# A two-layer language-model tower: quantised feed-forward and recurrence rebuilt as three streaming blocks, weights rounded beside the attention, expert mixture in quarters

## What is computed

```python
x = emb[inp]                        # token attention, then a second "spin" attention
# quantised feed-forward
scale = sigmoid(clip_x) * max(abs(x)) / 127         # one number for the whole tensor
xq = clip(round(x / scale), -128, 127) * scale
gate, up = xq @ q(w_gate).T, xq @ q(w_up).T         # q(): a scale for each row of w
h  = silu(gate) * up                                # 704 wide, then quantised like x
y  = h_q @ q(w_down).T
# recurrence with a mixture of 8 experts
x = inputs * rsqrt(mean(inputs * inputs) + 1e-6) * norm_weight
probs = softmax(mean(x, axis=1) @ router_w.T + router_b)   # one row for each sequence
W_hg, W_out = einsum(probs, w_hg), einsum(probs, w_out)
hidden, gate = split(x @ W_hg.T)                    # then the scan over 1024 steps
h_t = (1 - sigmoid(gate_t)) * h_{t-1} + sigmoid(gate_t) * g(hidden_t)
out = h @ W_out.T + inputs
# then 6 layers of local attention (16 heads, window 64) and a gated feed-forward
```

## Time and profile before

| | us |
|---|---|
| median of 3 runs (lowest, highest) | 4348.81 (4348.57, 4349.60) |
| the profiled execution, its own time | 4352.46 |
| its span in the profile | 4350.7 |
| second attention's last context | 1048.99 |
| scale of x known | 1121.02 |
| scale of h known | 1171.29 |
| shares of the experts known | 1262.67 |
| X for the local layers ready | 1367.27 |
| local layers' first matmul | 1375.30 |

### The profile page before, as it was taken

The page is one execution under the profiler, slowest core; times in us unless marked ns, Lnnn a source line. Parts: engine busy times, 40 slices in busy tenths (PEclk is TensorE's granted clock), DMA queues, the critical chain, the costliest instruction groups (busy, mean ns, idle before and its releaser), DMA issues. The chain is left out here.

```text
span 4350.7 us, 98162 instructions
## 1 busy us (share of the span) xinstructions
PE 4037.7 (93%) x33170; PEld 2814.9 (65%) x33172; DVE 3164.0 (73%) x5506; ACT 2640.2 (61%) x7021; POOL 1908.4 (44%) x1269
## 2 busy tenths in 40 slices
PE   6999979997426999999999999999999999999997
PEld 3666546664113677777777777777777777777776
DVE  4888448885865777777777777777777777777774
ACT  2677536774302666666666666666666666666664
POOL 1000000000002666666656666665666666566662
PEclk8999989999668999999999999999999999999999
DMA  6111141221022100111002100111002100111001
GB/s 154 40 44 44 23 114 44 55 55 32 0 69 96 23 20 19 50 45 27 20 19 61 39 20 21 49 45 27 20 19 60 40 19 21 49 47 25 20 19 49
DMA packets 102633, 178.80 MB, mean 41 GB/s; under 512 B 26756, under 2 KB 61472, under 8 KB 101792
## 3 DMA queue, kind: packets, MB, share of 16 engines
q1 hardware_dynamic: 101408, 170.87, 14.7%
q0 software_dynamic: 768, 2.10, 0.3%
HBM read 96.10 MB, written 23.07 MB: 27 GB/s over the span
## 5 line engine op out<-in xcount | busy, mean ns | idle before, releaser
L1855 POOL TENSOR_TENSOR swp<-raw,table 128x512 f32<-128x512 f32 x384 | 480.8, 1274 | 638.9 <-DVE ss L2266 638.8
L1017 DVE TENSOR_REDUCE maxima<-PS 128x1 f32<-128x512 f32 x1024 | 632.2, 680 | 123.8 <-PE PS L851 123.3
L1938 PE MATMUL PS<-wqk,xT 128*128 128x512 f32 x1536 | 687.7, 601 | 5.6 <-DMA wqk<-in_L_ffn_Wqkv 4.4
L1885 POOL TENSOR_TENSOR probs<-probs,prob_recip 128x512 f32<-128x512 f32 x384 | 476.4, 1260 | 430.4 <-DVE prob_recip L2324 430.4
L981 ACT ACTIVATE probs<-PS 128x512 f32<-128x512 f32 x1024 | 520.0, 603 | 155.2 <-PE PS L865 154.7
L2195 ACT ACTIVATE probs<-probs,neg 128x128 f32<-128x128 f32 x1536 | 595.9, 389 | 27.2 <-DVE neg L2318 25.7
L1865 POOL TENSOR_TENSOR rinv<-ssm,power 128x32 f32<-128x32 f32 x96 | 526.8, 5488 | 0.0
L1938 PEld LDWEIGHTS PS<-wqk,xT 128*128 128x128 f32 x1536 | 284.0, 190 | 336.8 <-issue 254.1
L2041 PE MATMUL PS<-xnT,w 128*128 128x128 f32 x3840 | 477.3, 276 | 0.4 <-DVE hidden L2384 0.4
L851 PE MATMUL PS<-k_stack,q_stack 112*128 112x512 f32 (+1 forms) x1024 | 430.8, 442 | 35.0 <-PEq L384 18.5
L2266 DVE TENSOR_REDUCE ss<-swp 128x16 f32<-128x1024 f32 x192 | 232.9, 1213 | 304.8 <-ACT swp L2146 304.8
(11 more groups left out here) (255 smaller groups left out, 8029.7 us busy)
## 6 DMA issues: line engine op xcount, KB each, us to landing
V_window<-V SPq DMA_DIRECT2D x180, 256.0 KB, 2.8
wqk<-in_L_ffn_Wqkv SPq DMA_DIRECT2D x12, 1024.0 KB
w<-in_L_ffn_W SPq DMA_DIRECT2D x18, 640.0 KB, 4.4
q_stack<-spin_qk SPq DMA_DIRECT2D x128, 80.0 KB
k_stack<-spin_qk SPq DMA_DIRECT2D x128, 80.0 KB
q_stack<-tok_qk SPq DMA_DIRECT2D x128, 64.0 KB
k_stack<-tok_qk SPq DMA_DIRECT2D x128, 64.0 KB
wv<-in_L_ffn_Wqkv SPq DMA_DIRECT2D x6, 1024.0 KB, 5.0
```

The source lines that it names most:

```text
L1017: dve.tensor_reduce(maxima[:, k // 2, k % 2:k % 2 + 1], SM(r, k), AX.X, ALU.max).then_inc(sm_maxed, 1)
L1855: pool.tensor_tensor(swp[:, w, :, a:a + LD // 2], raw[:, w, :, b:b + LD // 2], table[:, j % 2, 2 + w, a:a + LD // 2].rearrange("p (o d) -> ...
L1885: pool.tensor_tensor(view, view, psr[:, 4 * q:4 * q + 4].rearrange("p (h o) -> p h o", o=1) .to_broadcast([P, 4, P]), ALU.mult).then_inc(p ...
L1938: mm = pe.matmul(wide(kind, half, j), xT[:, k, at:at + P], rhs, start=(k == 0), stop=(k == DC - 1))
```

## The change

The chain of blocks between the second attention and the local layers becomes three blocks. `join_outputs` does the output projection, the layer norm, the peak and the turning of the weights; `feed_forward` does the quantised feed-forward, the layer norm, the second norm and the router; the new `recurrence` mixes, scans, projects, normalises and spills. In each, pairs of tiles or chunks pass from engine to engine.

- Weights: `QuantisedWeights` keeps 3072 + 1408 columns of weights; `beside` hooks in `attend` load them (SP, step 5), add the output bias to H (POOL, step 5), take the exponential of the clips (ACT, step 33) and round them (DVE, `round`, ahead of step 34). The last subtraction goes to ACT in `join_outputs`.
- Quantising h: ACT scales it and adds the rounding constant (1536 columns for a pair of tiles), DVE clips (L1536), ACT takes the constant off.
- POOL adds the down projection to H, computes both standard deviations from the moments (six small operations for each pair), and joins H and X.
- The router's weights are turned on the host, its logits come from PE; norm_weight goes into the experts' shares.
- Mixture: `w_hg` is mixed a quarter at a time by DVE (`mix(n)` for unit n: 2 + 14 operations of 2x128 columns), `w_out` by ACT (products) and POOL (14 sums of 128x512). The first unit's matmuls wait for its quarter only.
- All eight experts' weights are loaded at the start of `feed_forward`.
- One of the five cleanups goes; the one after the first attention moves to behind the second attention's projections.

```diff
+        with nc.cleanup_on_exit():
+            with ExitStack() as weights:
+                m = QuantisedWeights(c, weights, shared)
+                attend(c, V, qs, ks, second, spin_loaded, context, HD + 4, {
+                    "pool": {0: lambda pool: m.clear(c, pool), RING - 1: lambda pool: m.add_bias(c, pool, w["next"]["bo"])},
+                    "sp": {RING - 1: lambda sp: m.load(c, sp)},
+                    "act": {ITERS + 1: lambda act: m.exponent(c, act)},
+                    "dve": {ITERS + 2: lambda dve: m.round(c, dve)}})
+                join_outputs(c, context, w["next"]["wo"], m)
...
     def over_heads(eng, step, last, others):
...
+            if t in others:
+                others[t](eng)
...
+def join_outputs(c, context, wo, m):
...
+            @block.vector
+            def _(dve):
...
+                for ch in range(CHUNKS):
+                    add_output(2 * ch)
+                    add_output(2 * ch + 1)
+                    count(ch)
+                    if ch:
+                        norm(ch - 1)
+                norm(CHUNKS - 1)
...
+def feed_forward(c, m, x):
...
+            @block.gpsimd
+            def _(pool):
+                pool.memset(hT[64:P, IC - 1, :], 0.0).then_inc(cleared, 1)
...
+                def add_output(g):
+                    pool.wait_ge(out_scaled, g + 1)
+                    at = slice(PAIR * g, PAIR * g + PAIR)
+                    pool.tensor_tensor(c.H[:, at, :], c.H[:, at, :], scaled_out[:, g % 2, :, :], ALU.add).then_inc(ffn_added, 1)
...
+                def join(g):
+                    at = slice(PAIR * g, PAIR * g + PAIR)
+                    pool.wait_ge(normed, PAIR * g + PAIR)
+                    pool.tensor_tensor(c.H[:, at, :], c.H[:, at, :], c.X[:, at, :], ALU.add).then_inc(h_joined, 1)
+
+                for g in range(PAIRS + 1):
+                    if g < PAIRS:
+                        add_output(g)
+                        deviations(g)
+                    if g:
+                        join(g - 1)
...
+                for g in range(PAIRS + 2):
+                    if g + 1 < PAIRS:
+                        to_integers(g + 1)
+                    if g < PAIRS:
+                        round_h(g)
+                    if g >= 2:
+                        norm_again(g - 2)
...
+                for g in range(PAIRS + 3):
+                    if g < PAIRS:
+                        clip_h(g)
+                    if 1 <= g <= PAIRS:
+                        count(g - 1)
+                    if g < PAIRS:
+                        scale_output(g)
+                    if 1 <= g <= PAIRS:
+                        norm(g - 1)
+                    if g >= 3:
+                        take_normed(g - 3)
...
+def recurrence(c, x, spilled):
...
+                        pool.tensor_tensor(x.mixed_out[:, b, :, :], x.mixed_out[:, b, :, :], product[:, n % 2, :, :], ALU.add).then_inc(summed, 1)
...
+                mix(0)
+                mix(1)
+                mix(2)
+                scan(0)
+                mix(3)
+                scan(1)
+                scan(2)
+                scan(3)
...
-            attentions(c)
+            shared = c.sb(first, "shared", [P, 6 * CH])
+            m = attentions(c, shared)
             with nc.cleanup_on_exit():
-                quantised_ffn(c, lambda: layernorm(c, c.H, c.X))
-                recurrence(c, lambda: layernorm(c, c.H, c.X))
-            with nc.cleanup_on_exit():
-                spill(c, c.H, spilled, lambda: layernorm(c, c.H, c.X))
+                with ExitStack() as ctx:
+                    x = Mixture(c, ctx)
+                    feed_forward(c, m, x)
+                    recurrence(c, x, spilled)
```

More of the change, by code:

```diff
@@ L59, in wait @@
     eng.wait_ge(sem, value)
[L62 to L93, removed]
@@ L701, in attentions @@
             token_projections(c, V, qs, ks, first, loaded, w, s)
[L702 removed]
+            attend(c, V, qs, ks, first, loaded, context, HD, {})
+            spin_projections(c, V, qs, ks, second, spin_loaded, context, w, s, shared)
+        spin.close()
         with nc.cleanup_on_exit():
[L704 to L706 removed]
@@ L745, in attend @@
+    return m
+def attend(c, V, qs, ks, scratch, loaded, context, rows, beside):
     nc = c.nc
@@ L789, in misc_free, with over_heads @@
                 return
-    def over_heads(eng, step, last):
+    def over_heads(eng, step, last, others):
         for t in range(RING):
+            if t in others:
+                others[t](eng)
             step(t, t, 0)
@@ L827, in step @@
                     load(h0)
-            over_heads(sp, step, 3)
+            over_heads(sp, step, 3, beside.get("sp", {}))
         @block.gpsimd
@@ L840, in step @@
                     take_values(h0)
-            over_heads(pool, step, 0)
+            over_heads(pool, step, 0, beside.get("pool", {}))
         @block.tensor
@@ L958, in step @@
                     score_for_max(h0, 7)
-            over_heads(pe, step, 4)
+            over_heads(pe, step, 4, beside.get("pe", {}))
         @block.scalar
@@ L1007, in step @@
                     take_output(h2)
-            over_heads(act, step, 2)
+            over_heads(act, step, 2, beside.get("act", {}))
         @block.vector
@@ L1066, in step @@
                     maximum(h0, 15)
-            over_heads(dve, step, 4)
+            over_heads(dve, step, 4, beside.get("dve", {}))
     ctx.close()
@@ new lines, in logits @@
+                def logits(b):
+                    pe.wait_ge(mean_ready, DC * b + DC)
+                    pe.wait_ge(weighted, DC)
+                    wait(pe, routed, b)
+                    for k in range(DC):
+                        mm = pe.matmul(c.PS[:, 7, 0:E], spread[:, k, :], rw[:, 1, k, :], start=(k == 0), stop=(k == DC - 1))
+                    mm.then_inc(logits_done, 1)
+                pe.wait_ge(cleared, 3)
+                turn(0)
+                for ch in range(CHUNKS):
+                    for j in range(IC):
+                        gate_up(IC * ch + j)
+                        if j == 1 and ch + 1 < CHUNKS:
+                            turn(ch + 1)
```

1089 lines of the change are left out of this document (656 added, 433 removed).

## The result

| | before | after | forecast |
|---|---|---|---|
| median of 4 runs (lowest, highest), us | 4348.69 (4347.11, 4349.60) | 4293.89 (4291.31, 4301.61) | 4269 (4242 to 4293) |
| profiled execution: time, span | 4352.46, 4350.7 | 4291.31, 4289.4 | |
| head 31's context to scale of x | 72.0 | 31.2 | 31.7 |
| to scale of h | 50.3 | 52.6 | 46.5 |
| to the shares | 91.4 | 78.1 | 80.2 |

The ratio is 0.9877 with a 95% interval of 0.986 to 0.9894. The kernel got faster by 54.8 us where 79.5 were forecast, and the time lies 0.9 us above the range. The table shows two misses: the way to the scale of h, 6.1 us longer than forecast, and the local layers, 18.2 us longer although no line of them changed.

The account below looks back on a forecast made before the run. Ahead of the local layers no engine is full: a chain of DVE work and waits for barriers, DMA issue or POOL. Gains of 40.3 + 3.8 + 11.2 + 24.2 = 79.5 us gave 4269.3 at the median; range 4242 to 4293.

Parts of the forecast that it names:

- The local layers: Part after X: begins as now, 1.8 us behind X, and waits for its own loads; no change.
- a part behind X that is not 2983 us long: Sign that the forecast is wrong: the local layers' part not lasting 2983 us, as now.
- its own case of 4258 to 4281: Whole kernel: the prediction's main case, given 55%, 4258 to 4281 us by its own terms.
- The scale of x: From head 31's context to the scale of x: 72.0 us falls to 31.7, a gain of 40.3.
- 1070.4: Within the way to the scale of x: the time in us when TensorE's last pair is out.
- The scale of h: From scale of x to scale of h: 50.3 us falls to 46.5, a gain of 3.8.
- The term of 24 products, eight maxima and two clips: DVE's work on the way to the scale of h: 32.9 us, plus 1 for TensorE's slow start.
- The shares: From scale of h to the shares: 91.4 us falls to 80.2, a gain of 11.2.
- from there POOL sets the pace: On the way to the shares, after the first pair: POOL's chain sets rounds of 8.6 us, seven taking 60.2.
- To X: From shares to X: 104.6 us falls to 80.4 with most port waits counted, a gain of 24.2.
- port waits are rare: Rival, 22%: DVE and POOL seldom block each other in pair rounds, the fourth part and the memset; 4246 us.
- POOL's small operations are dear: Rival, 18%: six small operations queue behind DVE's norms, a round grows by up to 3.5 us; 4294 us.

Follow-up runs that it names:

- after + 64: 64 extra semaphore instructions on TensorE ahead of its first matmul in the recurrence block, against the kernel after: 4276.25 us, ratio 0.9834.
- Experiment 3: Against after with 64 extra TensorE instructions: memset of hT behind the fourth clip, all four x clips done at once, silu table loaded at block start: 4263.96 us.
- experiment 4: Against after with 64 extra TensorE instructions: DVE clips h one pair ahead of where it did: 4266.96 us, ratio 0.9807.
- experiment 2: Against after with 64 extra TensorE instructions: without POOL's 14 w_out sums, 4263.14 us; separately, hT memset delayed until the second x clip, 4272.75 us.

## Why the prediction was wrong

**The local layers.** "The local layers begin as now, 1.8 us behind X, and wait for their own loads: nothing." This step failed, by 18.2 us. They did begin 79.5 us earlier as forecast, but by luck: 74.6 within the marks, where all 79.5 should have been, 4.3 ahead of them, 0.7 at the boundary. They wait for nothing that the kernel's text shows, but four jumps back whose instructions came late cost 20.3 us, where before is 1.9 above after + 64. The sentence "a part behind X that is not 2983 us long" stood among the signs of a wrong forecast, rightly, but no rival had a mechanism for it. With 64 instructions more the time is 4276.25: 7 us from the forecast, inside its own case of 4258 to 4281. The 6.1 us of the scale of h are still in it.

**The scale of x.** Right to 0.5 us, though its 1070.4 doesn't follow from its terms (1049.3 + 3.4 + 7 x 2.3 is 1068.8). POOL's reduce came 5.79 us behind the free engine, the library's time:

```profile
1075.07 0.38 POOL L1121 PARTITION_ALL_REDUCE peak<-peak  x1 [5.79 <-issue]
```

**The scale of h.** The start was right: boundary, clip beside the memset and first product at 1087.42, 11.5 us behind the scale where 11.3 were forecast. The term of 24 products, eight maxima and two clips, 32.9 (its own numbers give 32.4), "plus 1 us for TensorE's slow start", measured 40.3: DVE was busy 33.2, but stood idle for 7.1 where the term had 1. A chain of DVE work was summed as if nothing fed it late. In the kernel after, the clip of the third chunk stands between the fifth and the sixth product of the first; ACT waited 0.64 us for it and TensorE 1.36 for ACT. TensorE's clock over the stretch was 0.84. Experiment 3 has 3.4 us idle left, at clock 1.00.

**The shares.** The number held (78.1 for 80.2, rounds of 8.4 for 8.6), the reason did not: "from there POOL sets the pace" is refuted by experiment 4. The sum came out right by luck. It shares with the real ring POOL's addition or the norm beside it, the copy and the clip. The rest of it, statistics, small operations and join (5.1 us), happens to weigh what the ring has in their place, ACT's rounding, TensorE's projection and DVE's scaling (1.48 + 3.08 + 0.69 = 5.25).

**To X.** Right to 1.4 us, and here the reason too: DVE lost 14.0 us to port waits (experiment 2), where the sum had 15.8 and took 13.8. The rival "port waits are rare" is out for the mixture (5.62 against 12.70 us); "POOL's small operations are dear" is out as well, as they take 0.2 to 0.7 us in after.

**The start.** Head 31's context came 4.3 us earlier, which the sum had no term for. In the twelve profiles of kernels with after's front, that context's operation starts between 1043.9 and 1055.6 us, in the two with before's front at 1048.4 and 1048.7. Two of the twelve lie 5 us or more behind the ten others, and in them TensorE's clock from 500 to 600 us was 0.90, where the ten others have 0.98 to 1.00. So the 4.3 us are not the change's for certain, and a few us in the medians of this section are of this kind.

## What to carry to other kernels

After any change ahead of a hardware loop that fills TensorE, look at the waits of that loop for "issue" at its jump, and at the jump instruction's own time, in the part that was not touched: a shift of the code alone moved this kernel by 20 us, 0.5%, and 64 idle instructions in a place where TensorE waits took it back. When a sum is made of one engine's operations, ask of each what feeds it, and follow the idle times in brackets once around before calling an engine the one that sets the pace. And put sums on POOL only where DVE isn't in a long row of operations with two SBUF inputs.

## What the hardware showed that I had not expected

- A jump back in TensorE's program takes its sequencer 3.3 to 4.3 us in every run here, and matmuls issued ahead cover it. At some places a second wait of 3.1 to 3.4 us follows; it cost 2.6 us of standing still and about as much again behind it. The place counts modulo 256 instructions: the layers last 2999.8, 2979.7, 2979.3, 2979.7, 2999.9 us with 0, 64, 128, 192, 256 more.
- DVE and POOL do not always take turns. In one run a sum of POOL waited out 28 additions of DVE and lasted 13.2 us; in after, with DVE first as well, they alternated. The Trainium skill says in "SBUF — State Buffer", section "Who interferes with whom", of DVE's operations in the two-port mode, that whoever issues first gets the shared pair for the whole instruction; here, with additions of two SBUF inputs, it was once for a whole row of instructions.
- A semaphore instruction took 0.154 us on TensorE (64 more of them, 9.8 us more to the first unit).
